# The first part of a recurrent block with routed experts, in another order: transpositions and router logits ahead of most gates of the second sequence

## What is computed

```python
def reference(x, ...):
    xn = _layernorm(x)
    return x + _L0_attn_ref(xn, ...) + _L0_ffn_ref(xn, ...)

def _L0_attn_ref(x, ...):
    h = _rmsnorm(x, pre_norm_w)
    a = sigmoid(h @ w_a + decay_bias)          # decay
    i_gate = sigmoid(h @ w_i)
    v = h @ w_v
    input_signal = sqrt(clip(1.0 - a * a, 1e-08)) * (i_gate * v)
    rec_out = _chunked_scan(a, input_signal)   # s[t] = a[t] * s[t-1] + input_signal[t]
    x = x + rec_out @ out_proj_w
    h2 = _rmsnorm(x, ffn_norm_w)
    gate, up = split(h2 @ w_gate_up, 2)
    return x + silu(gate) * up @ w_down

def _L0_ffn_ref(x, w_router, w_fc, w_proj):    # 8 experts, the best 2 of each token
    top_vals, top_idx = top_k(x_flat @ w_router, 2)
    probs = softmax(top_vals)
    # each token: sum over its two experts of prob * (relu(x @ w_fc[e]) ** 2) @ w_proj[e]
```

## Time and profile before

| | |
|---|---|
| median of 3 runs | 336.8 us (336.75 to 338.13) |
| the profiled execution's own time | 335.52 us |
| its span in the trace | 333.8 us |
| PE busy | 295.5 us, 89% of the span |
| DVE busy | 200.8 us, 60% |
| ACT busy | 171.5 us, 51% |
| POOL busy | 156.3 us, 47% |
| mean granted clock of PE | 0.958 of full |

### The profile page before, as it was taken

One profiled execution on the slowest core, in us unless ns is written; L12 is line 12 of the kernel. 1 busy time (PEld: TensorE's weight loads), 2 busy tenths in 40 slices (PEclk: granted clock), 3 DMA queues, 4 the chain that ended last, 5 costly groups with the idle time before them and its releaser, 6 DMA issues.

```text
span 333.8 us, 5643 instructions
## 1 busy us (share of the span) xinstructions
PE 295.5 (89%) x1842; PEld 260.8 (78%) x1842; DVE 200.8 (60%) x460; ACT 171.5 (51%) x361; POOL 156.3 (47%) x130
## 2 busy tenths in 40 slices
PE   6589979957685889799899998999999989999993
PEld 6568868746574778698799997889999778888882
DVE  2277747889998984368845555884565552343332
ACT  2669737726836333664336557443655752222220
POOL 5523121500860335748765866786586664316000
PEclk9779979979969899979999999999999999999999
DMA  6999910007030102433433444334443452919931
GB/s 218 355 385 372 422 62 0 0 2 196 0 111 17 34 16 51 65 50 51 66 64 65 65 66 66 64 63 67 67 64 66 64 62 34 165 26 156 226 124 64
DMA packets 31228, 34.29 MB, mean 103 GB/s; under 512 B 5088, under 2 KB 28896, under 8 KB 31168
## 3 DMA queue, kind: packets, MB, share of 16 engines
q0 software_dynamic: 11712, 14.58, 27.7%
q1 hardware_dynamic: 16560, 17.25, 15.2%
q10 hardware_dynamic: 2928, 2.10, 2.0%
HBM read 22.06 MB, written 13.96 MB: 108 GB/s over the span
## 4 chain that ended last, share of the span: by engine, by line
PE 72%; DVE 15%; ACT 4%; issue 3%; DMA 2%; POOL 2%; SPq 1%; DVEq 0%; ACTq 0%; POOLq 0%
PE ps L353 60%; PE ps L411 5%; PE ps L545 4%; DMA X<-in_L_attn_x_dram 2%; PE ps L379 2%; ACT h L704 1%; DVE at_lane L1018 1%; PE ps L424 1%; DVE hT_lo L887 1%; DVE gu L1064 1%; PE ps L362 1%; DVE one_of L1028 1%; DVE dec L921 1%; DVE nblk L984 1%; DVE h2T_lo L936 1%
## 5 line engine op out<-in xcount | busy, mean ns | idle before, releaser
L1281 POOL DMA_INDIRECT xg<-xh_dram,gather_u x39 | 49.5, 1270 | 55.4 <-DVE picks L1094 30.5
L1290 POOL DMA_INDIRECT acc_dram<-yb,gather_u x39 | 62.4, 1599 | 15.2 <-issue 8.6
L353 PE MATMUL ps<-h2T_lo,Wgu_hi 128*128 128x512 f32 x128 | 43.4, 400 | 0.0
L353 PE MATMUL ps<-Wd_hi,guT_hi 128*128 128x256 f32 x128 | 37.2, 291 | 6.8 <-DVE guT_lo L1069 6.8
L353 PE MATMUL ps<-h2T_hi,Wgu_hi 128*128 128x512 f32 x128 | 40.8, 400 | 0.7 <-DVE h2T_lo L936 0.7
L1064 DVE TENSOR_TENSOR gu<-gu,ps 128x512 f32<-128x512 f32 x32 | 21.9, 685 | 30.9 <-PE ps L353 30.8
L353 PE MATMUL ps<-h2T_hi,Wgu_lo 128*128 128x512 f32 x128 | 40.2, 396 | 0.0
L353 PE MATMUL ps<-Wd_hi,guT_lo 128*128 128x256 f32 x128 | 37.0, 289 | 0.0
L353 PE MATMUL ps<-Wd_lo,guT_hi 128*128 128x256 f32 x128 | 37.0, 289 | 0.0
L724 ACT ACTIVATE gu<-ps 128x512 f32<-128x512 f32 x32 | 19.1, 597 | 34.1 <-PE ps L353 34.0
L1111 DVE TENSOR_TENSOR aT_lo<-ps,aT_hi 128x256 fp32r<-128x256 f32 x39 | 16.5, 424 | 27.4 <-ACT aT_hi L754 25.1
(11 more groups left out here) (167 smaller groups left out, 691.6 us busy)
## 6 DMA issues: line engine op xcount, KB each, us to landing
X<-acc_dram POOLq DMA_DIRECT2D x8, 512.0 KB, 9.1
acc_dram<-zero SPq DMA_DIRECT2D x1, 2176.0 KB, 14.3
X<-in_L_attn_x_dram SPq DMA_DIRECT2D x4, 512.0 KB, 8.0
Wgu_raw<-in_L_attn_w_gate_up_dram SPq DMA_DIRECT2D x4, 512.0 KB, 9.8
xh_dram<-X ACTq DMA_DIRECT2D x4, 512.0 KB, 7.5
Wfc_raw<-in_L_ffn_w_fc_dram SPq DMA_DIRECT2D x4, 512.0 KB, 11.5
Wpj_raw<-in_L_ffn_w_proj_dram SPq DMA_DIRECT2D x4, 512.0 KB, 4.0
out_dram<-X SPq DMA_DIRECT2D x3, 512.0 KB, 6.1
```

The lines of the kernel that those rows point to most:

```text
L353: return nc.tensor.matmul(dst, lhs, rhs, start=start, stop=stop, skip_group_check=group)
L1281: pool.indirect_dma_start(out=xg[i % XG][:, :], out_offset=None, in_=xh_dram, in_offset=bass.IndirectOffsetOnAxis(ap=gather_u[:, i:i + 1], ...
L1290: pool.indirect_dma_start(out=acc_dram[i % 2], in_=yb[i % YB][:, :], in_offset=None, compute_op=ALU.add, out_offset=bass.IndirectOffsetOnA ...
```

## The change

- A third place for hT: sequence c uses its own tiles at (place 0, the space of h2T[0], place 1, place 0). Only `split_h(3)` still waits, for the six gate tiles of sequence 0. The gains of sequences 1 and 2 move to the other half of `Wpj_hi`.
- `normalise_x(2)` and `normalise_x(3)` go from ACT to DVE, as four tensor_scalar instructions each (subtract the mean, multiply with the reciprocal root). `xh_ready` becomes one semaphore for each sequence.
- PE: transpositions and logits come earlier between the gate tiles; `count` stands ahead of sequence 2's gate tiles, `transpose_h2(0, ...)` behind all six of them.
- ACT: `split_h(0)` and `copy_xh(0)` ahead of `normalise_x(1)`, the other `split_h` and `copy_xh` earlier, `weights_hi(3)` to `(5)` ahead of `squares(0)`.
- DVE: `take_logits` and `top_two` directly behind the recurrence of sequence 0; `add_residual(0, ...)` behind `take_counts`.

```diff
-        hT = [(put(f"hT{u}_hi", [P, K, S], F32R, at), put(f"hT{u}_lo", [P, K, S], F32R, at + 4 * KB))
-              for u, at in enumerate((Wpj_hi_at, Wpj_hi_at + 8 * KB))]
...
+        hT = [(put(f"hT{c}_hi", [P, K, S], F32R, at), put(f"hT{c}_lo", [P, K, S], F32R, at + 4 * KB))
+              for c, at in enumerate((Wpj_hi_at, h2T_at[0], Wpj_hi_at + 8 * KB, Wpj_hi_at))]
...
-                for b, at in enumerate((cum_at, Wpj_hi_at, Wpj_hi_at + 4 * KB, cum_at))]
+                for b, at in enumerate((cum_at, Wpj_hi_at + 8 * KB, Wpj_hi_at + 12 * KB, cum_at))]
...
             keep_clock(24, 7)
-            for n in range(4):
-                aiv(0, n)
+            aiv(0, 0)
+            aiv(0, 1)
             transpose_x(1)
+            aiv(0, 2)
+            aiv(0, 3)
+            logits(0)
             aiv(0, 4)
             aiv(0, 5)
-            logits(0)
+            transpose_x(2)
             aiv(1, 0)
+            logits(1)
             aiv(1, 1)
-            transpose_x(2)
-            for n in range(2, 4):
-                aiv(1, n)
-            logits(1)
-            for n in range(4, 6):
-                aiv(1, n)
             transpose_x(3)
             logits(2)
+            aiv(1, 2)
+            logits(3)
+            aiv(1, 3)
             output_projection(0, 0)
             output_projection(0, 1)
-            logits(3)
-            for n in range(4):
+            aiv(1, 4)
+            aiv(1, 5)
+            count()
+            for n in range(6):
                 aiv(2, n)
-            count()
             transpose_h2(0, 0)
             transpose_h2(0, 1)
-            aiv(2, 4)
-            aiv(2, 5)
...
             def split_h(c):
                 act.wait_ge(xT_done, c + 1)
                 if c == 0:
                     act.wait_ge(small_loaded, 48)
-                if c >= 2:
-                    act.wait_ge(aiv_done, 6 * (c - 1))
+                if c == 3:
+                    act.wait_ge(aiv_done, 6)
...
             normalise_x(0)
             store_xh(0)
-            normalise_x(1)
             split_h(0)
             copy_xh(0)
+            normalise_x(1)
             store_xh(1)
             decay(0, 0)
             decay(0, 1)
-            normalise_x(2)
+            split_h(1)
+            copy_xh(1)
             input_gate(0, 0)
             input_gate(0, 1)
-            split_h(1)
+            store_xh(2)
             decay_squares(0)
+            split_h(2)
             gains(0)
-            copy_xh(1)
-            store_xh(2)
-            normalise_x(3)
+            copy_xh(2)
+            store_xh(3)
+            split_h(3)
+            copy_xh(3)
             decay(1, 0)
             decay(1, 1)
-            split_h(2)
-            copy_xh(2)
-            store_xh(3)
+            weights_hi(3)
             input_gate(1, 0)
             input_gate(1, 1)
-            split_h(3)
-            copy_xh(3)
-            weights_hi(3)
+            weights_hi(4)
+            weights_hi(5)
             squares(0)
-            weights_hi(4)
-            normalise(0)
             decay(2, 0)
             decay(2, 1)
-            weights_hi(5)
+            normalise(0)
...
+            def normalise_x(c):
+                dve.wait_ge(rstd_ready, c + 1)
+                for j in range(J):
+                    t = J * c + j
+                    last = V.tensor_scalar(X[c][:, j, :], X[c][:, j, :], mv[:, t, 0:1], rn1[:, t:t + 1],
+                                           ALU.subtract, ALU.mult)
+                last.then_inc(xh_ready[c], 1)
...
             statistics(3)
+            normalise_x(2)
             split_h(1)
+            normalise_x(3)
+            scales()
             gated_value(0, 0)
             gated_value(0, 1)
-            scales()
+            split_h(2)
             signal(0, 0)
             signal(0, 1)
             cumulate(0, 0)
             recur(0, 0)
-            split_h(2)
+            split_h(3)
             cumulate(0, 1)
             recur(0, 1)
-            split_h(3)
+            take_logits()
+            top_two()
             gated_value(1, 0)
             gated_value(1, 1)
+            take_counts()
             add_residual(0, 0)
             add_residual(0, 1)
-            take_logits()
-            top_two()
-            take_counts()
             place_tokens()
             split_h2(0)
```

More of the change, by code:

```diff
@@ L204, in recurrent_moe_block @@
         dve_chain, pool_chain = sem("dve_chain"), sem("pool_chain")
-        var_ready, rstd_ready, xh_ready = sem("var_ready"), sem("rstd_ready"), sem("xh_ready")
+        var_ready, rstd_ready = sem("var_ready"), sem("rstd_ready")
+        xh_ready = [sem(f"xh_ready{b}") for b in range(B)]
         xh_stored = [sem(f"xh_stored{b}") for b in range(B)]
@@ L366, in transpose_x @@
             def transpose_x(c):
-                pe.wait_ge(xh_ready, c + 1)
+                pe.wait_ge(xh_ready[c], 1)
                 if c:
@@ L395, in aiv @@
                     for k in range(K):
-                        last = product(ps[:, rec_bank(b, n), :], Waiv[l][:, k, col:col + P], hT[b % 2][h][:, k, :],
+                        last = product(ps[:, rec_bank(b, n), :], Waiv[l][:, k, col:col + P], hT[b][h][:, k, :],
                                        m + k == 0, m == 2 and k == K - 1)
@@ L648, in normalise_x @@
                                         bias=nb1[:, t:t + 1])
-                last.then_inc(xh_ready, 1)
+                last.then_inc(xh_ready[c], 1)
             def store_xh(c):
-                act.wait_ge(xh_ready, c + 1)
+                act.wait_ge(xh_ready[c], 1)
                 act.dma_start(xh_t[c], X[c][:, :, :]).then_inc(xh_stored[c], 16)
@@ L658, in split_h @@
                     act.wait_ge(small_loaded, 48)
-                if c >= 2:
-                    act.wait_ge(aiv_done, 6 * (c - 1))
+                if c == 3:
+                    act.wait_ge(aiv_done, 6)
                 for k in range(K):
-                    A.activation(hT[c % 2][0][:, k, :], ps[:, TX + k, :], ACT.Copy,
+                    A.activation(hT[c][0][:, k, :], ps[:, TX + k, :], ACT.Copy,
                                  scale=pre_w[:, k:k + 1]).then_inc(hT_hi, 1)
@@ L886, in split_h @@
                     dve.wait_ge(hT_hi, K * c + k + 1)
-                    V.scalar_tensor_tensor(out=hT[c % 2][1][:, k, :], in0=ps[:, TX + k, :], scalar=pre_w[:, k:k + 1],
-                                           in1=hT[c % 2][0][:, k, :].bitcast(F32), op0=ALU.mult,
+                    V.scalar_tensor_tensor(out=hT[c][1][:, k, :], in0=ps[:, TX + k, :], scalar=pre_w[:, k:k + 1],
+                                           in1=hT[c][0][:, k, :].bitcast(F32), op0=ALU.mult,
                                            op1=ALU.subtract).then_inc(hT_split, 1)
```

## The result

The change is faster. Its executions took 324.66, 326.43 and 322.48 us, median 324.66, beside 336.97 us (336.75 to 338.13) for the kernel before: ratio 0.9624, interval 0.9546 to 0.9702. A second comparison of the same two kernels gave 325.22 us (322.42 to 326.53) against 335.75 us, ratio 0.970, 0.9667 to 0.9733. So the gain is 10.5 to 12.3 us by the medians, in either comparison more than the 9.5 us forecast.

The account below looks back on a forecast made before the run. Bound by a chain mostly through PE up to the counts, then DVE's queue to the first expert products, then PE. -9.7 + 0.9 - 0.7 = -9.5 us gave 326.0 against the profiled execution, 327.3 by median; range 325.0 to 331.5.

Parts of the forecast that it names:

- Step 1: First gate tile on PE: starts at 15.4 us instead of 18.17, 2.8 us earlier, without having waited.
- Step 2: Clock during PE's first 24 products: stays full instead of falling to half, 1.7 us gained; other bound 0.
- Step 3: PE up to the fourth logits: two waits, for copies, and the logits end at 39.4 us instead of 53.3.
- Step 4: Fourth logits to counts: 1.6 us charged for half clock, counts taken at 49.3 us against 59.01, minus 9.7.
- Step 5: Counts to h2T_lo: POOL's subtractions hold DVE's small instructions, h2T_lo starts at 59.3 us, plus 0.9.
- literal reading: Within step 5: nothing else is held by POOL, so h2T_lo starts at 55.9 us, 3.4 us sooner.
- rival A: The hold is escaped, by the literal reading or POOL starting 1.8 us later: 323.9 us; chance 10%.
- Step 6: h2T_lo to first expert products: DVE's waits for PE in gated values shrink, minus 0.7, bounds 0 to minus 1.6.
- B: Logits' chain through ACT and DVE comes later, bringing PE waits and half clock: about 331.5 us; chance 17%.
- C: Half clock through the first part, 15 to 49 us, some 14 us slower: 341 us; chance 4%.
- D: No gain: a place or semaphore ties sequences together, or DVE meets a fixed-time wait: 336 to 338 us; chance 3%.
- Step 7: Moves at no cost: DVE's eight normalising instructions run under cover; without it they would cost up to 2 us.

Follow-up runs that it names:

- start_undone: Changed kernel with ACT's first split and copy put back behind the normalisation of sequence 1: 328.91 us, ratio 0.9809 to the kernel before.
- dve_order: Changed kernel with the blocks' places and two lanes moved ahead on DVE behind the counts, POOL's subtractions left in place: 326.61 us, ratio 0.9714.
- start_only: Kernel before, with only ACT's first split and copy moved ahead of the normalisation of sequence 1: 331.58 us, ratio 0.9883.
- after_again: Changed kernel run again without an edit: 325.22 us, ratio 0.970 to the kernel before.
- pool_early: Changed kernel with POOL's two weight subtractions released by the routing gap, ahead of the residual's root: 325.2 us, ratio 0.9682.
- kept_clock: Changed kernel with 24 constant products on PE ahead of the fourth logits: 322.52 us, ratio 0.962.
- norms_on_act: Changed kernel with the third and fourth sequences' normalisations back on ACT: 332.67 us, ratio 0.9899.
- pool_dve_clock: Changed kernel with POOL's pair released earlier, blocks' places and two lanes ahead on DVE, and 24 constant products before the fourth logits: 322.3 us, ratio 0.9633.
- all_four: Changed kernel with earlier first normalisation and split, 24 constant products, POOL's pair released earlier and DVE's new order: 321.54 us, ratio 0.9551.

## Why the prediction was right in its places and short in its size

*Step 1* gave 2.8 us; the first gate tile came 4.0 us earlier. The two profiled executions differ already at the first transposition, 11.45 against 10.15 us, because a cast of ACT waited for the weights in the one and not in the other. ACT's timeline of before:

```profile
8.12 1.32 ACT L641 ACTIVATE Waiv_hi<-Waiv_raw 128x512 fp32r<-128x512 f32 x2 [1.11 <-DMA Waiv_raw<-in_L_attn_w_i_dram]
9.34 2.06 ACT L647 ACTIVATE X<-X,nb,rn 128x256 f32<-128x256 f32 x4
```

That is chance, not the change: start_undone has its transposition at 11.56, dve_order at 11.51. In dve_order's profile, with the late transposition, the first gate tile starts at 15.22 us without a wait, as the step said (15.4): the reasoning held for the case it took, and the other 1.2 us come of the kind of start that the profiled execution happened to have. The step treated the 11.45 and the half clock behind it (24 constant products in 2.77 us, elsewhere 1.50) as fixed. What replaced PE's constants as the last thing was the decay's bias, landing at 11.92 us, which the step did not name.

*Step 2* held: full clock from 14 to 37 us. With step 1 it makes 4.5 us; start_only and start_undone both measure about 4.

*Step 3* held to 0.2 us: fourth logits end at 39.3 against 39.4, with the two waits it named. The 1.2 us gained in step 1 did not get through, since here PE waits for ACT and DVE.

*Step 4* held: the counts were taken at 49.14, forecast 49.3 (minus 9.87 against minus 9.7), with the half clock in the place charged. The size is that of this execution: the fall stood elsewhere in after_again and lasted 10.2 us in pool_early, and its removal (kept_clock) is worth 2.7 us by the medians, more than the 1.6 charged.

*Step 5* was right about the hold and wrong about the path. h2T_lo started at 59.19 against 59.3, plus 0.95 us against plus 0.9, so the literal reading, and rival A with it, falls: both subtractions held what DVE issued into them. That agrees with the Trainium skill (SBUF — State Buffer, Who interferes with whom), whose rule the step followed, at 1.82 and 2.31 us. Not everything is held, though. Into POOL's earlier subtraction (40.75 to 43.12 us) DVE issued a reduction and then a comparison, and only the second was held:

```profile
40.85 0.29 DVE L963 TENSOR_REDUCE first<-tmp 128x16 f32<-128x128 f32 x1
41.17 2.09 DVE L964 TENSOR_TENSOR mask<-rank,first 128x128 f32<-128x128 f32 x1
```

And the path was wrong: pool_early took the hold away and won nothing. In the changed kernel PE's twelve gate tiles and a transposition, up to 65.88 us, end later than what DVE has to do, by the 0.40 us that DVE waits at 65.97; the plus 0.9 of the sum was off the path. The 3.4 us of the literal reading could not have come either: without the hold h2T_lo is bound by the transposition behind six gate tiles, and came 1.1 us sooner (pool_early), which the step did not see.

*Step 6* is the term of the sum that failed by its size. From h2T_lo to the first expert products it was 38.26 us before and is 36.39 now: minus 1.87, where I took minus 0.7 and a bound of minus 1.6. The stretches of both kernels show why (the columns as above; of before, then of the changed kernel):

```profile
68.11:106.37 38.26, 26.24 (x142) 21.71 (x143) 35.89 (x49) 22.80 (x31) 12.89 (x7) 0.87 0.26 71
```
```profile
59.19:95.58 36.39, 26.39 (x154) 21.89 (x153) 35.68 (x49) 26.90 (x40) 12.87 (x7) 0.92 0.27 75
```

DVE is busy nearly as long as before, 35.9 and 35.7 us; its idle time fell from 2.4 to 0.7 us. I had counted only the gated values' waits, 1.6 us, and taken less than half of them. They fell to 0.40, minus 1.2; a wait of 0.43 us for PE ahead of a later product (L1064 at 99.46 in before) went too, and DVE was busy 0.2 less. As I read it the late h2T_lo, with PE at work all the while, is what lets PE be there first; no run tests that alone. Steps 5 and 6 should have been one term, worked out as the later of PE's queue and DVE's.

*Sum.* Minus 9.87, plus 0.95, minus 1.87 is minus 10.8 us at the first expert products, and minus 10.9 at the end, against minus 9.5. *The conversion* "1.3 us higher by the median" was the other loss in the first comparison: the profiled execution of before was quicker than the others of that comparison (335.52 against 336.75 and more), that of after stood in the middle of its own (324.66). In the second comparison the forecast's own ratio, 327.3 over 336.8 or 0.972, lies inside the measured 0.9667 to 0.9733. The range gave too little room below: its low end took one term at a time, while two bounds (no fall in step 4, all of step 6) can come together, which makes 324.8, and executions of one kernel are 4 us apart.

*Rivals.* B happened only when provoked (norms_on_act). C did not: after 14 us the clock fell once before the counts, and the longest fall there with the change's own order was 10.2 us of some 36 (pool_early). D is excluded by every comparison. A's 323.9 us is near the result, with the wrong mechanism; that would have been luck.

*Step 7* held: DVE normalises in 1.38 us for four instructions at 18.81 and 22.11 us, under cover. But what it frees on ACT is worth 2.3 us at least, which no step had as a term of its own.

## What to carry to other kernels

Where two queues meet behind a stretch, work out both ends and take the later, instead of adding what each gained: a stall of 3.8 us on DVE cost nothing here, until its idle time was filled, and then 1.5 to 2.5. A PE wait beside 8-column products can be dear beyond its length, so price it as the wait plus a slow stretch, give that stretch a wide range (3.4 to 10 us here for the same instructions), and try constant products in it before anything else. And read a start-up time from several executions, not from one: what hangs on the arrival of a transfer moved by 1.3 to 1.5 us from one profile to the next.

## What I had not expected of the hardware

- 24 products of constants, 1.5 us of work that computes nothing, made the program 2.7 us shorter (kept_clock). Whether they also narrow its spread is not shown: 2.0 us over four executions, but pool_early without them has 1.9 over four, and pool_dve_clock with them 4.0 over six.
- PE can stay at 1.2 GHz while it is busy without a gap (norms_on_act, 10.00 of 10.00 us at a granted 0.50). And one and the same sequence of instructions up to the counts was at that level for 3.4 us from 39 us on in one execution, for as long from 33.8 us on in another (after_again), and for 10.2 us in a third (pool_early).
- A subtraction on POOL holds even a 128x4 instruction of DVE: 1.20 us for what takes 0.17 elsewhere (all_four at 12.44 us). A reduction of 128x128 issued into such a subtraction took its usual 0.29 us (the change at 40.85).
